# Third stage of a vision-tower kernel: row statistics one step ahead and in halves, the routed rows' transposes in another bank, norm steps in another order

## The reference

```python
def _ln(x, g, b):                       # last step of layer 0's routed feed-forward
    m = jnp.mean(x, axis=-1, keepdims=True)
    v = jnp.mean((x - m) ** 2, axis=-1, keepdims=True)
    return (x - m) / jnp.sqrt(v + 1e-05) * g + b
...
    x = _ln(moe + x, ln3_g, ln3_b)      # moe: two experts of eight per token, weighted
...
h = h + _L0_ffn_ref(_layernorm(h, axis=-1), ...)
h = h + _L1_attn_ref(_layernorm(h, axis=-1), ...)   # 8 heads, window of 32 keys to each side
h = h + _L1_ffn_ref(_layernorm(h, axis=-1), ...)    # one of 16 experts per image, softmax gate
```

## Time and profile before

| | us |
|---|---|
| three runs: median (lowest to highest) | 2887.75 (2885.34 to 2888.98) |
| the profiled execution, as a run | 2891.1 |
| its span in the trace | 2888.0 |
| PE busy | 2576.3 (89%) |
| PE weight loads, beside PE | 2032.2 (70%) |
| DVE busy | 2083.3 (72%) |
| ACT busy | 1803.9 (62%) |
| POOL busy | 1033.2 (36%) |

### The profile page before, as it was taken

How to read it: one execution, slowest core, us unless ns; L and a number is a source line. 1 busy time by engine, 2 the same in 40 slices (tenths; PEclk the granted TensorE clock), 3 DMA queues, 4 the chain that set the end, 5 groups by cost and what they waited for, 6 DMA issues and landing times.

```text
span 2888.0 us, 71290 instructions
## 1 busy us (share of the span) xinstructions
PE 2576.3 (89%) x25177; PEld 2032.2 (70%) x25177; DVE 2083.3 (72%) x6017; ACT 1803.9 (62%) x3853; POOL 1033.2 (36%) x916
## 2 busy tenths in 40 slices
PE   6998999999898988499999997899999999999996
PEld 4666666666666665399999996676677776667765
DVE  3788888888888888455555554577777777777775
ACT  3777767767777776344444443566766676666674
POOL 1355555555555555455555554101110111000100
PEclk9999999999999999699999998999999999999998
DMA  3222222222222211377777775121112211122110
GB/s 136 70 83 84 85 83 82 83 83 89 87 98 84 87 60 35 107 233 229 228 235 228 228 233 171 39 67 51 51 51 61 65 51 51 51 62 62 51 34 29
DMA packets 135788, 288.40 MB, mean 100 GB/s; under 512 B 22752, under 2 KB 79072, under 8 KB 131424
## 3 DMA queue, kind: packets, MB, share of 16 engines
q1 hardware_dynamic: 113504, 245.36, 27.9%
q0 software_dynamic: 22016, 39.43, 4.2%
HBM read 215.79 MB, written 68.92 MB: 99 GB/s over the span
## 4 chain that ended last, share of the span: by engine, by line
PE 62%; DVE 20%; ACT 12%; issue 4%; DMA 1%; POOL 1%; SPq 0%; DVEq 0%; ACTq 0%; POOLq 0%
PE psum L513 15%; PE psum L1190 9%; PE psum L1181 9%; PE psum L519 4%; PE psum L1592 3%; PE psum L1535 3%; PE psum L1552 3%; ACT nrows L1752 3%; PE psum L1540 2%; ACT ex L1788 2%; DVE acc L816 2%; PE psum L1605 2%; PE psum L1575 2%; ACT r L1758 2%; ACT r L1760 2%
## 5 line engine op out<-in xcount | busy, mean ns | idle before, releaser
L1225 ACT ACTIVATE hid<-psum,w_blk 128x256 f32<-128x256 f32 x608 | 268.9, 473 | 325.0 <-PE psum L1181 325.0
L1047 POOL DMA_INDIRECT expert_in<-rows,slot_i x384 | 376.7, 981 | 157.0 <-issue 140.6
L1788 ACT ACTIVATE ex<-psum,smin 128x80 f32<-128x80 f32 x1152 | 281.1, 331 | 206.9 <-DVE smin L1874 206.8
L1153 POOL DMA_INDIRECT expert_out<-rows_out,dest x304 | 291.0, 957 | 290.5 <-DVE rows_out L1320 242.3
L513 PE MATMUL psum<-xn,w_in 128*128 128x288 f32 x1024 | 313.5, 432 | 31.6 <-ACT rf L726 27.6
L1190 PE MATMUL psum<-w_blk,hid 128*128 128x128 f32 x2432 | 297.2, 276 | 0.0
L1181 PE MATMUL psum<-x_t,w_blk 128*128 128x256 f32 x1216 | 289.6, 382 | 2.2 <-DMA w_blk<-w_exp_in 2.2
L1190 PEld LDWEIGHTS psum<-w_blk,hid 128*128 128x128 f32 x2432 | 284.4, 193 | 0.1
L1514 POOL TENSOR_TENSOR x2c<-x2c,ycho 96x768 f32<-96x768 f32 x32 | 57.7, 1802 | 611.4 <-DMA ycho<-expert_out 611.4
L513 PEld LDWEIGHTS psum<-xn,w_in 128*128 128x128 f32 x1024 | 192.0, 200 | 99.3 <-DVE xn L874 40.4
L1017 POOL TENSOR_TENSOR unit<-unit 128x576 f32<-128x576 f32 x64 | 120.0, 1875 | 354.9 <-ACT unit L680 272.7
(11 more groups left out here) (259 smaller groups left out, 5789.8 us busy)
## 6 DMA issues: line engine op xcount, KB each, us to landing
w_blk<-w_exp_in SPq DMA_DIRECT2D x152, 578.5 KB
xin<-x_in SPq DMA_DIRECT2D x32, 1716.0 KB, 7.1
rows_in<-expert_in SPq DMA_DIRECT2D x152, 132.0 KB
ycho<-expert_out SPq DMA_DIRECT2D x64, 288.0 KB, 5.3
h_dram<-h SPq DMA_DIRECT2D x32, 288.0 KB, 2.1
x_dram<-rows SPq DMA_DIRECT2D x32, 288.0 KB, 3.2
h1c<-h_dram SPq DMA_DIRECT2D x32, 288.0 KB, 4.4
x2c<-x_dram SPq DMA_DIRECT2D x32, 288.0 KB, 5.2
```

Of the source, the lines that this page charges most:

```text
L1047: pool.indirect_dma_start(out=expert_in[:, :], out_offset=bass.IndirectOffsetOnAxis(ap=slot_i[z.s][:, n:n + 1], axis=0), in_=rows[z.s][:, ...
L1153: pool.indirect_dma_start(out=expert_out[:, :], out_offset=bass.IndirectOffsetOnAxis(ap=dest[b.s][:, c:c + 1], axis=0), in_=rows_out[b.s][ ...
L1225: nc.scalar.activation(hid[b.s][:, c, :], HB[b.s][c % HK], ACT.Gelu_apprx_tanh, bias=w_blk[b.q][:, FF + FC * D + c:FF + FC * D + c + 1]).t ...
L1788: done = nc.scalar.activation(ex[u][:, b, in_window(qb)], score_bank(u)[:, b * QK:(b + 1) * QK], ACT.Exp, bias=smin[u % RING][:, b:b + 1], ...
```

## The change

- `ysum` and `halves3` get two buffers each, by item parity; POOL's second sum waits for `nrows` of two items back.
- `row_halves` moves from item `w` to item `v`, so to the end of the step before, in two calls of three `bn_stats`: one behind `pick_expert`, one behind `residual` and ahead of `xq`.
- `normed_rows` is two calls of three activations, with `exps(x, 3)` between them, and both behind `inverse_root(y)` and `turned(x, 2)`; `row_root` follows `turned(x, 0)`.
- `moe` goes into A0 behind `turn(x, 3)` and `values(x, 2)`, and waits for the logarithm of `inverse_root(y)` in place of `xm`. The router's logits go into A1. `centre` of `w` follows the router at once and waits for `pick_expert`'s first instruction; `turn(x, 4)` and `scores(x, 7)` follow it, then `project` of `sq4`, then `values(x, 4)`.
- On DVE `h2` comes ahead of `minimum(x, 5)`, `residual(z)` behind `minimum(x, 7)`, `minimum(x, 1)` ahead of `row_stats`. On ACT `square(w)` comes ahead of `turned(x, 4)`, `inverse_root(w)` ahead of `turned(x, 5)`.

```diff
-        ycho, ysum = pair_c("ycho", [G, 2, NG, D]), one_c("ysum", [G, NG, D])
-        halves3, stats = one_c("halves3", [G, NG, 6]), one_c("stats", [G, NG, 2])
+        ycho, ysum = pair_c("ycho", [G, 2, NG, D]), pair_c("ysum", [G, NG, D])
+        halves3, stats = pair_c("halves3", [G, NG, 6]), one_c("stats", [G, NG, 2])
...
-                if x.old(1):
-                    pool.wait_ge(nrows_ready, x.upto(1, 0))
-                pool.tensor_tensor(ysum[:], x2c[x.s][:], ycho[x.s][:, 1, :, :], ALU.add).then_inc(ysum_step, 1)
+                if x.old(2):
+                    pool.wait_ge(nrows_ready, x.upto(2, -2))
+                pool.tensor_tensor(ysum[x.s][:], x2c[x.s][:], ycho[x.s][:, 1, :, :], ALU.add).then_inc(ysum_step, 1)
...
                     scores(x, 4)
+                    turn(x, 3)
+                    values(x, 2)
                 if w:
                     if y:
-                        pe.wait_ge(xm_ready, y.upto(1, 1))
+                        pe.wait_ge(norm5_act, y.upto(3, 2))
...
-                    moe(w, A1)
-                if x:
-                    turn(x, 3)
-                    values(x, 2)
...
+                    moe(w, A0)
                 if x:
                     scores(x, 5)
                     values(x, 3)
                     scores(x, 6)
                 if y:
-                    router(y, A0)
+                    router(y, A1)
+                if w:
+                    pe.wait_ge(h2_ready, w.upto(1, 1))
+                    if y:
+                        pe.wait_ge(pick_step, y.upto(PICK, 1))
...
+                    centre(A1, w, h2).then_inc(norm4_pe, 1)
                 if x:
                     turn(x, 4)
                     scores(x, 7)
                 if w:
-                    pe.wait_ge(h2_ready, w.upto(1, 1))
-                    centre(A1, w, h2).then_inc(norm4_pe, 1)
+                    pe.wait_ge(norm4_act, w.upto(3, 1))
+                    project(A0, C("mean"), sq4[:]).then_inc(norm4_pe, 1)
                 if x:
                     values(x, 4)
                     turn(x, 5)
...
+                if y:
+                    inverse_root(y, r5, A0, norm5_pe, norm5_act)
+                if x:
+                    turned(x, 2)
                 if w:
-                    normed_rows(w)
-                if y:
-                    inverse_root(y, r5, A0, norm5_pe, norm5_act)
-                if x:
-                    turned(x, 2)
+                    normed_rows(w, 0)
+                if x:
                     exps(x, 3)
+                if w:
+                    normed_rows(w, 1)
...
                 if y:
                     pick_expert(v, y)
+                if v_:
+                    row_halves(v_, 0)
                 if x:
                     halves(x, 4)
-                if z:
-                    residual(z)
-                if x:
                     heads(x, 4)
                     minimum(x, 7)
+                if z:
+                    residual(z)
+                if v_:
+                    row_halves(v_, 1)
```

More of the change, by code:

```diff
@@ L1543, in moe @@
             def moe(x, bank):
-                pe.wait_ge(nrows_ready, x.upto(1, 1))
+                pe.wait_ge(nrows_ready, x.upto(2, 2))
                 for g in range(NG):
@@ L1716, in step @@
                     turn(x, 5)
-                if w:
-                    if y:
-                        pe.wait_ge(pick_step, y.upto(PICK, 1))
-                    elif x:
-                        pe.wait_ge(k_ready, x.upto(1, 1))
-                    pe.wait_ge(norm4_act, w.upto(3, 1))
-                    project(A0, C("mean"), sq4[:]).then_inc(norm4_pe, 1)
-                if x:
                     scores(x, 8)
                     turn(x, 6)
-                if x:
                     values(x, 5)
@@ L1750, in normed_rows @@
                     act.wait_ge(moe_done, x.upto(1, 0))
-                for g in range(NG):
-                    last = nc.scalar.activation(nrows[:, g, :], ysum[:, g, :], ACT.Identity, bias=move3[:, g:g + 1],
+                for g in range(k * NG // 2, (k + 1) * NG // 2):
+                    last = nc.scalar.activation(nrows[:, g, :], ysum[x.s][:, g, :], ACT.Identity, bias=move3[:, g:g + 1],
                                                 scale=root3[:, g:g + 1])
@@ L1820, in step @@
                     exps(x, 1)
+                if x:
+                    turned(x, 0)
                 if w:
                     row_root(w)
-                if x:
-                    turned(x, 0)
                 if y:
@@ L1840, in step @@
                     exps(x, 5)
-                    turned(x, 4)
                 if w:
@@ L1844, in step @@
                 if x:
+                    turned(x, 4)
                     exps(x, 6)
-                    turned(x, 5)
                 if w:
@@ L1849, in step @@
                 if x:
+                    turned(x, 5)
                     exps(x, 7)
@@ L1890, in heads, with row_halves @@
                                 one_head[:], inv[:], ALU.mult).then_inc(att_ready, 1)
-            def row_halves(x):
-                v.wait_ge(ysum_step, x.upto(YSUM, YSUM))
-                for g in range(NG):
-                    last = v.bn_stats(halves3[:, g, :], ysum[:, g, :])
+            def row_halves(x, k):
+                if k == 0:
+                    v.wait_ge(ysum_step, x.upto(YSUM, YSUM))
+                for g in range(k * NG // 2, (k + 1) * NG // 2):
+                    last = v.bn_stats(halves3[x.s][:, g, :], ysum[x.s][:, g, :])
                 last.then_inc(halves3_ready, 1)
             def row_stats(x):
-                v.wait_ge(halves3_ready, x.upto(1, 1))
+                v.wait_ge(halves3_ready, x.upto(2, 2))
                 if x.old(1):
@@ L1903, in row_stats @@
                 for g in range(NG):
-                    last = v.bn_aggr(stats[:, g, :], halves3[:, g, :])
+                    last = v.bn_aggr(stats[:, g, :], halves3[x.s][:, g, :])
                 last.then_inc(stats_ready, 1)
@@ L1945, in step @@
                     pick_gate(v, z)
-                if w:
-                    row_halves(w)
                 if y:
@@ L1950, in step @@
                     heads(y, 8)
+                if x:
+                    minimum(x, 1)
                 if w:
                     row_stats(w)
-                if x:
-                    minimum(x, 1)
                 if z:
@@ L1983, in step @@
                     v.tensor_reduce(means[:], four(xm[:]), AX_X, ALU.add).then_inc(means_ready, 1)
-                if x:
-                    minimum(x, 5)
                 if w:
@@ L1988, in step @@
                     v.wait_ge(h_landed[w.s], 16 * w.n + 16)
-                    v.scalar_tensor_tensor(out=two(h2[:, w.s * T:(w.s + 1) * T]), in0=both(A1), scalar=V("ln3_g"),
+                    v.scalar_tensor_tensor(out=two(h2[:, w.s * T:(w.s + 1) * T]), in0=both(A0), scalar=V("ln3_g"),
                                            in1=two(h1c[w.s][:]), op0=ALU.mult, op1=ALU.add).then_inc(h2_ready, 1)
                 if x:
+                    minimum(x, 5)
                     halves(x, 3)
@@ L1996, in step @@
                     pick_expert(v, y)
+                if v_:
+                    row_halves(v_, 0)
                 if x:
                     halves(x, 4)
+                    heads(x, 4)
+                    minimum(x, 7)
                 if z:
                     residual(z)
-                if x:
-                    heads(x, 4)
-                    minimum(x, 7)
+                if v_:
+                    row_halves(v_, 1)
                 if w:
@@ L2017, in pick_expert @@
             v.wait_ge(router_done, x.upto(1, 1))
-            v.scalar_tensor_tensor(out=l16[:], in0=A0[0:NI, 0, 0:E2], scalar=1.0 / S, in1=RR("bg")[0:NI, :],
+            v.scalar_tensor_tensor(out=l16[:], in0=A1[0:NI, 0, 0:E2], scalar=1.0 / S, in1=RR("bg")[0:NI, :],
                                    op0=ALU.mult, op1=ALU.add).then_inc(pick_step, 1)
```

10 lines of the change are left out of this document (6 added, 4 removed).

## The result

| | us |
|---|---|
| before, three runs and those beside the changed kernel: median (lowest to highest) | 2887.68 (2885.34 to 2888.98) |
| changed kernel, four runs | 3015.03 (3001.42 to 3025.57) |
| ratio, with its 95% interval | 1.0439 (1.0391 to 1.0488) |
| span of the changed kernel's profiled execution | 3023.4 |

Slower, as forecast, but by 127 us instead of 70, and above the upper end of the range. The profile of the changed kernel shows the waits that the prediction named, and two things that its sum did not count: a lower clock and a wait for `gdiag`.

The account below looks back on a forecast made before the run. PE, busy 184.16 of 200 us, was taken as the bound, so gains come only from its waits. Per full step +2.5 - 0.51 + 0.35 = +2.3, 29 steps +67, with the first two steps +70: 2958 us, range 2925 to 3004.

Parts of the forecast that it names:

- The transposes no longer wait for `xm`, but PE meets `turn(x, 3)` instead: On PE at `turn(x, 3)`: idle some 1.75 us for `exps(x, 3)` instead of 1.34 for `xm`; no gain.
- the centring, queued behind the pick: At `centre` on PE: waits some 1.7 us for DVE's pick instruction, with `turn(x, 4)` and `scores(x, 7)` queued behind; `values(x, 4)` 2.68 later.
- `xq` behind `values(x, 4)`: At the step's end on DVE: `xq` starts 2.5 us later, including 0.62 for the second half of `row_halves`.
- The sum of these at full clock: Per full step of the third stage: the new order makes `xq` start 2.5 us later, entered as +2.5.
- `att` and the POOL sums: At DVE's `att` beside POOL's two back-to-back sums: a wait of 0.35 us per step in place of 0.51.
- the clock: Rival, PE's longer pauses: clock falls cost 1.6 us per slip, 3004 with one each step, 2974 with one in three; chance 0.15.
- The first steps: The two steps before the full ones: about +1 and +2 us; filling, draining and the first two stages 0.
- Faster: Rival: DVE answers the router at once, ACT has `exps(x, 3)` ready, PE loses three waits: -68 us, 2820; chance 0.05.
- It comes out even: Rival: PE's later work hides the pick wait, +0.4 against -0.5 per step, 2885; chance 0.03.
- the replay is too harsh: Rival: the replay's joints, off in one direction, take 1.0 of the 2.3 per step: +41 us, 2929; smaller losses 0.05.

Follow-up runs that it names:

- b_banks: Kernel before with only the banks exchanged (`moe` into A0 without the wait for `xm`, router into A1, `centre` waits for the pick): ratio 1.0062 to before.
- e1: Changed kernel plus eight products per step that nobody reads, placed in PE's three pauses: ratio 1.0331 to the kernel before.
- e3: Changed kernel with `centre` again behind `turn(x, 4)` and `scores(x, 7)`, `project` behind `turn(x, 5)`, ACT's calls as before: ratio 1.0142 to the kernel before.
- e4: Changed kernel with all six `bn_stats` behind the pick, none ahead of `xq`: ratio 1.0334 to the kernel before.
- c1_three: Changed kernel with POOL's sums behind `att`, `centre` back behind `scores(x, 7)`, and all `bn_stats` behind the pick: 2914.91 us, ratio 1.0096 to the kernel before.
- c2_tight: c1_three with `exps(x, 3)` ahead of both `normed_rows`, `turned(x, 3)` ahead of `exps(x, 4)`, `moe` and `h2` later: ratio 0.9887 to the kernel before.
- c1_fill: c1_three plus three spare products ahead of `turn(x, 3)`: 2998.96 us beside 2992.60 for the kernel before, ratio 1.0022.
- e2_pool_late: Changed kernel with POOL's two sums waiting for the last `att` of item `y`: ratio 1.0320 to the kernel before.

## Why the prediction was wrong in size, step by step

**Right: "The transposes no longer wait for `xm`, but PE meets `turn(x, 3)` instead".** 1.75 of idle time was forecast, 1.89 found, and b_banks shows the exchange of waits by itself (1.34 for 1.45).

**Right: the centring, queued behind the pick, and `xq` behind `values(x, 4)`.** The pick's wait is 1.21 in the mean instead of 1.7. It is 1.77 in the 12 steps where the clock hadn't fallen ahead of it, and 0.68 to 0.95 in the 17 where it had; in e1, at full clock, the pause with its filling is 1.78. e3 shows that this move is what costs most. `xq`'s wait is 1.10 ("over 1.0"), of which e4 gives 0.57 to the three `bn_stats`.

**The sum of these at full clock** is e1's 3.05 less what `att` and `gdiag` do in it (`att` 0.12 for 0.53, `gdiag` 0.84): 2.62 per step. The prediction had +2.5, which is 3 us short over the 29 steps. (Its 0.51 per step for `xq` in the kernel before divides 16 waits by 15 steps; the wait is 0.47. Nothing in the sum hangs on it.)

**Wrong: "`att` and the POOL sums", -0.51 + 0.35 per step.** Which instruction the sums would meet was placed wrongly. The prediction reckoned them against the `att` of unit 8, 1 to 2.4 into the 3.6 us. But they begin 7.2 us behind `xq` where the first one began at 9.7 before (medians of the 29 steps), 2.4 earlier and not 1 to 2, and in most steps are over when that `att` comes (2229.92 in the step above, the sums end at 2228.99). They meet `att` of unit 7 with the first sum, for which PE doesn't wait, and `gdiag` with the second. `att` came out better than forecast (0.13), but `gdiag` costs 0.84 to 0.87. The term is +0.43 in place of -0.16: 0.6 a step, 17 us. The prediction looked only at the instruction that had waited before; it should have gone through every instruction of DVE in the 3.6 us. The Trainium skill, in SBUF — State Buffer, Who interferes with whom, puts under the same exclusive lock, beside the instructions with two SBUF inputs that the prediction cited, those that VectorE runs in a mode with two ports, and names `tensor_scalar` among the kinds that can where their operands meet the conditions. `gdiag` is one of that kind. If it runs in that mode it stands until the sum ends; the trace agrees, with 1.27 for 0.22, though it doesn't show the mode.

**Wrong: the clock, left out of the sum and given 0.15 as a rival.** The argument against it was that pauses of 1.35 left the clock at 1.00. That was true of those pauses, and it holds in b_banks (1.45, 3.4 us at half rate); it says nothing of longer ones. With one of 1.91 the clock falls in 22 of 29 steps (c1_three); with two or three long pauses in a step it falls in 26, and in six of them more than once (the changed kernel's first trace). e1 puts the cost at 1.0 to 1.4 per step, 30 to 39 us. The rival's own price was near that, 1.6 for each slip; it was its chance that was too low. And it stood alone in its case, while the range's upper end, 3004, left no room for it and for POOL's sums at once. The profiled execution closes so, on its span: 2958 + 39 (clock) + 17 (POOL's sums) + 3 (the rest of the order) + 5 (the first steps, below) = 3022, and the span is 3023.4. The median, 3015.03, lies lower by what executions of this kernel differ in. Without the clock, or without POOL's sums, it would have been inside the range (2976 to 2985, or 2998).

**The first steps** cost 6 and the start of the stage 3, where +3 was forecast for the steps and 0 for the start; the tail gives 2 back. That is 5 more than forecast, and its cause wasn't looked into.

**The rivals.** "Faster": the wait for `xm` was never worth its 1.35, since ACT's exponentials are due at the same time; b_banks excludes it for the exchange of the banks. But the premise of the case, that "ACT had `exps(x, 3)` ready", can be made nearly true by order alone (0.79 of waiting is left), and c2_tight with it gains 34 us, half of what that rival priced. "It comes out even" and "the replay is too harsh" are excluded by e1: at full clock the order costs 3.05 per step.

## What to carry to other kernels

Before a wait is removed, look up what the next instruction on that engine waits for: if another engine's work is due at the same moment, the wait only moves, and the piece to shift is that work. When several orders change at once, hold every new pause against those that the trace shows without a fall of the clock, and where it is longer, put the clock into the sum and not beside it. When a long POOL instruction moves, list all of DVE's instructions it will now meet, the tiny ones too: one of 16 numbers cost as much here as a large one.

## What the runs showed of the hardware that was not expected

**The clock and spare work.** Pauses up to 1.45 us (b_banks) left TensorE at 2.4 GHz in nearly all of the stage; with one of 1.91 in each step (c1_three) 75 us of 966 ran at 1.2 GHz. It isn't the sum of the idle time: PE stands idle 3.07 in a step of b_banks and 2.51 in one of c1_three. Nor is it the length of a single pause alone: in the kernel before, the clock fell behind waits for `att` of 1.28 and 1.17, not behind one of 1.34, and in b_banks behind one of 0.99. What else decides was not tried. Products that nobody reads, put in the pause, took the time at half rate to 0 (c1_fill) and made the program faster: by 23 us against c1_three, and by 26 to 38 in the changed kernel (e1_fill).

**POOL's add holds a tiny DVE instruction.** In the rows above `gdiag`, 4x4 and wholly in SBUF, takes 1.32 and ends with the sum; in e2_pool_late, away from the sums, 0.22. Beside the same two sums `one_head` (one operand in PSUM) took its 0.28, `smin` (from PSUM) its 0.48, and `g`, a reciprocal within SBUF, its 0.14. So being in SBUF alone doesn't make an instruction wait, and being tiny doesn't spare it the wait. Which property of `gdiag` decides was not tried by itself.
